# GpSimd's 512-column instructions in two parts each, and those of the weights' low halves in four

## The reference

```
x = x + 0.5 * ffn(layernorm(x), ...)
x = x + attn(layernorm(x), Wq, Wk, Wv, Wo, bo)
x = x + 0.5 * ffn(layernorm(x), ...)

attn: q, k, v = x @ Wq, x @ Wk, x @ Wv       # 32 query heads, 8 key/value groups, head size 128
      q, k = rope(q), rope(k)
      probs = softmax(where(causal, q @ k.T / sqrt(128), -inf))
      return (probs @ v) @ Wo + bo
ffn:  router scores of 128 slots, the best 8 kept, softmax over them, mixed values through two
      small matrices, times a gate made from a learned and a measured uncertainty; plus its input
```

## Time and profile before

| | |
|---|---|
| timed runs, median (lowest to highest) | 1462.56 us (1459.61 to 1463.27), 3 runs |
| the profiled execution, its own time | 1462.43 us |
| its span, first to last instruction | 1460.6 us |
| TensorE busy | 1384.1 us (95%) |
| VectorE busy | 1180.8 us (81%), 2816 instructions |
| ScalarE busy | 961.5 us (66%) |
| GpSimd busy | 721.1 us (49%), 603 instructions |
| mean granted TensorE clock | 0.978 of full |

### The profile page before, as it was taken

The page is one execution under the profiler, slowest core; times in us unless marked ns, Lnnn a source line. Parts: engine busy times, 40 slices in busy tenths (PEclk is TensorE's granted clock), DMA queues, the critical chain, the costliest instruction groups (busy, mean ns, idle before and its releaser), DMA issues.

```text
span 1460.6 us, 26285 instructions
## 1 busy us (share of the span) xinstructions
PE 1384.1 (95%) x8818; PEld 779.6 (53%) x8818; DVE 1180.8 (81%) x2816; ACT 961.5 (66%) x2423; POOL 721.1 (49%) x603
## 2 busy tenths in 40 slices
PE   5678999998999999999999999999999999999995
PEld 4335555554555655555555555555555555555543
DVE  6788968889988888889778788889777798868655
ACT  3467777676776766676766776666666777666733
POOL 0278766667765454435545354444543454344312
PEclk9699999999999999999999999999999999999997
DMA  7168766777767566656557566557565667464433
GB/s 234 44 165 205 192 158 175 191 178 196 176 144 173 135 126 134 138 119 153 129 128 167 127 134 145 119 131 141 139 138 136 135 146 161 120 141 103 98 76 116
DMA packets 439398, 210.54 MB, mean 144 GB/s; under 512 B 382016, under 2 KB 383232, under 8 KB 439264
## 3 DMA queue, kind: packets, MB, share of 16 engines
q1 hardware_dynamic: 437152, 204.66, 60.5%
q10 hardware_dynamic: 2112, 4.19, 0.9%
HBM read 90.30 MB, written 25.17 MB: 79 GB/s over the span
## 4 chain that ended last, share of the span: by engine, by line
PE 77%; DVE 11%; ACT 4%; issue 4%; POOL 3%; DMA 1%; DVEq 0%; SPq 0%; ACTq 0%
PE PJ L1191 17%; PE PJ L1193 17%; PE PJ L1192 17%; PE PV L1191 4%; PE PV L1193 4%; PE PV L1192 4%; PE SC L1357 4%; PE SC L1356 4%; PE SC L1355 4%; DVE phl L1008 3%; POOL t L530 2%; ACT p L685 2%; DVE p L998 2%; DVE t L971 1%; DVE t L969 1%
## 5 line engine op out<-in xcount | busy, mean ns | idle before, releaser
L538 POOL TENSOR_TENSOR oTl<-of,oTf 128x512 f16<-128x512 f32 x128 | 154.2, 1204 | 444.3 <-ACT oTf L677 444.2
L685 ACT ACTIVATE p<-p,mn 128x512 f32<-128x512 f32 (+3 forms) x512 | 280.8, 549 | 98.4 <-DVE mn L998 98.3
L1008 DVE SCALAR_TENSOR_TENSOR phl<-p,ri,phl 128x128 f16<-128x128 f32 (+3 forms) x512 | 333.2, 691 | 0.0
L1191 PE MATMUL PJ<-XT,wsp 128*128 128x512 f16 x640 | 244.4, 382 | 4.8 <-DVE t L971 1.7
L696 ACT ACTIVATE phl<-p,ri 128x128 f16<-128x128 f32 (+3 forms) x512 | 245.6, 550 | 4.1
L1192 PE MATMUL PJ<-XT,wsp 128*128 128x512 f16 x640 | 244.2, 382 | 0.0
L1193 PE MATMUL PJ<-XT,wsp 128*128 128x512 f16 x640 | 244.0, 381 | 0.0
L530 POOL TENSOR_TENSOR t<-t 128x512 f32<-128x512 f32 x160 | 204.7, 1279 | 72.8 <-DVE t L971 72.5
L998 DVE CUSTOM_DVE_ANT_0 p<-SC,maskw 128x512 f32<-128x512 f32 (+3 forms) x512 | 219.8, 485 | 2.1
L533 POOL TENSOR_TENSOR qTl<-t,qTh 128x512 f16<-128x512 f32 x128 | 148.4, 1159 | 93.2 <-ACT qTh L664 93.2
L1192 PE MATMUL PJ<-wosp,oTf 128*128 128x512 f16 x512 | 194.1, 379 | 0.0
(11 more groups left out here) (204 smaller groups left out, 2644.9 us busy)
## 6 DMA issues: line engine op xcount, KB each, us to landing
wsp<-kept SPq DMA_DIRECT2D x144, 256.0 KB, 3.0
wosp<-kept SPq DMA_DIRECT2D x96, 256.0 KB, 3.4
raw<-in_wqkv SPq DMA_DIRECT2D x48, 256.0 KB, 4.7
kept<-wsp SPq DMA_DIRECT2D x48, 256.0 KB, 2.4
raw<-in_wo SPq DMA_DIRECT2D x32, 256.0 KB, 4.7
kept<-wosp SPq DMA_DIRECT2D x32, 256.0 KB, 3.0
X<-in_x ACTq DMA_DIRECT2D x4, 1024.0 KB, 10.9
pTf<-phl SPq DMA_TRANSPOSE x256, 3.8
```

Of the source, the lines that this page charges most:

```text
L538: nc.gpsimd.tensor_tensor(oTl[:, n % 2, h, :], of[:, s % 2, :], oTh[:, n % 2, h, :], ALU.subtract).then_inc(o_lo, 1)
L685: ins = nc.scalar.activation(pt, pt, ACT.Exp, bias=mn[:, par, i:i + 1], scale=-1.0, accum_out=rs[:, par, i:i + 1])
L1008: nc.vector.scalar_tensor_tensor(out=phl[:, par, low(i, 0):low(i, i) + 1, :], in0=p[:, par, SOFF[i]:SOFF[i] + w].rearrange("p (k t) -> p k ...
L1191: mm(out_, lh, rh, start=start, stop=False)
```

## The change

Each GpSimd instruction over 512 columns is issued as several instructions over equal slices of the columns, one behind the other. The semaphore is raised by the last of them, so what waits for a tile waits for all of its parts, and the wait ahead of the tile is made once. Two parts of 256 columns are used for the bias addition, the low halves of normalized tiles, both rope instructions and the low half of the attention output; four parts of 128 columns for the weights. The penalty addition (L504) and the six additions at the very end (L573) stay whole. Data, order and waits stay as they are.

```diff
+            def parts(k):
+
+                return [slice(i * T // k, (i + 1) * T // k) for i in range(k)]
+
             def add_bias(bb, i):
...
-                nc.gpsimd.tensor_tensor(X[:, n, :], X[:, n, :], bob[:, :], ALU.add).then_inc(bo_add, 1)
+                for c in parts(2):
+                    ins = nc.gpsimd.tensor_tensor(X[:, n, c], X[:, n, c], bob[:, c], ALU.add)
+                ins.then_inc(bo_add, 1)
             def normal_lo(k, bb, i):
...
-                nc.gpsimd.tensor_tensor(both[:, C:2 * C], normal_of(k, bb, i), both[:, 0:C],
-                                        ALU.subtract).then_inc(ln_lo[k], 1)
+                hi, lo, x_ = both[:, 0:C], both[:, C:2 * C], normal_of(k, bb, i)
+                for c in parts(2):
+                    ins = nc.gpsimd.tensor_tensor(lo[:, c], x_[:, c], hi[:, c], ALU.subtract)
+                ins.then_inc(ln_lo[k], 1)
             def weight_low(r):
...
-                nc.gpsimd.tensor_tensor(w[:, 1, :], raw[:, r % NRAW, :], w[:, 0, :].bitcast(BF16),
-                                        ALU.subtract).then_inc(w_lo, 1)
+                for c in parts(4):
+                    ins = nc.gpsimd.tensor_tensor(w[:, 1, c], raw[:, r % NRAW, c], w[:, 0, c].bitcast(BF16), ALU.subtract)
+                ins.then_inc(w_lo, 1)
             def rope(kind, n, idx):
...
-                nc.gpsimd.tensor_tensor(t1[:, j, :], t1[:, j, :], t2[:, j, :], ALU.add).then_inc(rope_sum, 1)
+                for c in parts(2):
+                    ins = nc.gpsimd.tensor_tensor(t1[:, j, c], t1[:, j, c], t2[:, j, c], ALU.add)
+                ins.then_inc(rope_sum, 1)
...
-                nc.gpsimd.tensor_tensor(lo, t1[:, j, :], hi, ALU.subtract).then_inc(rope_lo, 1)
+                for c in parts(2):
+                    ins = nc.gpsimd.tensor_tensor(lo[:, c], t1[:, j, c], hi[:, c], ALU.subtract)
+                ins.then_inc(rope_lo, 1)
             def out_lo(s):
...
-                nc.gpsimd.tensor_tensor(oTl[:, n % 2, h, :], of[:, s % 2, :], oTh[:, n % 2, h, :],
-                                        ALU.subtract).then_inc(o_lo, 1)
+                for c in parts(2):
+                    ins = nc.gpsimd.tensor_tensor(oTl[:, n % 2, h, c], of[:, s % 2, c], oTh[:, n % 2, h, c], ALU.subtract)
+                ins.then_inc(o_lo, 1)
```

## The result

| | median us | lowest to highest | runs |
|---|---|---|---|
| before | 1461.09 | 1459.23 to 1463.27 | 4 |
| changed | 1471.11 | 1470.43 to 1471.62 | 4 |

The ratio is 1.0068, 95% interval 1.0054 to 1.0081: the change costs 10 us, where 3.5 us of gain had been forecast, and the time lies above the range of 1448 to 1468. In the changed kernel the lines of the earlier trace rows are 8 to 14 further down: L530 is now L540, L533 L545, L523 L532, L538 L552, L516 L524, and on VectorE L1008 is L1022, L844 L858 and L1102 L1116; TensorE's L1191 is L1205 and L1355 is L1369, ScalarE's L685 L699.

The account below looks back on a forecast made before the run. TensorE was taken as the bound, except before 440 us, where the loop through VectorE, GpSimd and ScalarE is as long or longer. The terms 3.8 + 0 - 7.5 + 0 + 0.2 = -3.5 us gave 1459 us, range 1448 to 1468.

Parts of the forecast that it names:

- The price of a part: On GpSimd, one more instruction adds 0.12 us, bounds 0 and 0.20; a halved instruction +0.12, a quartered one +0.36.
- Part 1: The start, 60 to 130 us: GpSimd is nearly the bound, so added instructions less idle time cost +3.8 us.
- Part 3: 250 to 440 us: shorter VectorE stalls shorten the steps and some granted clock returns, -7.5 us.
- the two chosen steps: Steps 335.88 to 348.01 and 322.93 to 335.88 us, forecast to shorten by 1.07 and 1.68 us.
- Part 2: 130 to 250 us: TensorE is the bound and GpSimd still has room, so nothing changes.
- Part 4: 440 to 1400 us: each query's rope way 0.24 us longer, TensorE busy throughout and not waiting, so nothing.
- Part 5: The end: L538 lies once before the last output products, +0.2 us.
- GpSimd becomes the bound of the early stage: Rival, chance 0.17: at 0.20 us a part, the start costs +8.4, 250 to 440 us gives -3.6: 1467 us.
- More relief: Rival, chance 0.26: a part costs only 0.05 us, start about +1, 250 to 440 us gains some 11.5: 1452 us.
- The parts do not let VectorE in: Rival, chance 0.09: GpSimd keeps its hold over the parts, stalls stay whole, only the cost is left: 1468 us.
- Hidden anyway: Rival, chance 0.06: the reciprocal waits for the exponentials and relief ends there: 1462 us.

Follow-up runs that it names:

- w4_alone: Kernel before with only the weights' low halves in four parts, everything else whole: 0.9975 of the time of the kernel before.
- w_cost_only: Kernel before with three memsets of 96 columns ahead of each weight's low half, which stays whole: ratio 1.0028 to the kernel before.
- w4_side2: Changed kernel with both rope instructions whole (weights in four; bias, normalized tiles, attention output in two): ratio 0.9999 to the kernel before.
- changed_rope_late: Changed kernel with rope sum and low half whole for the first 40 ropes, in two parts from then on: ratio 1.0009 to the kernel before.
- w2_alone: Kernel before with only the weights' low halves in two parts: 1453.07 us, ratio 0.9946 to the kernel before.
- rope2_alone: Kernel before with only the rope's sum and low half in two parts: ratio 1.0060 to the kernel before.
- side2_alone: Kernel before with only bias and low halves of normalized tiles and attention output in two parts: ratio 0.9994 to the kernel before.
- w2_side2: Kernel before with low halves of weights, normalized tiles and attention output, and bias, in two parts, rope whole: ratio 0.9972 to the kernel before.

## Why the prediction was wrong

**What held.** The price of a part was taken as 0.12 us, and is 0.14: a rope sum lasts 1.41 us against 1.27. The Trainium skill (GPSIMD Engine Reference, section Elementwise — side-by-side cycle accounting) led to an estimate of 0.17; the trace lies between the two. The parts do let VectorE in: L1022 fell to 757 ns, and w4_alone, faster than before where w_cost_only is slower, shows that this relief reaches the kernel's time.

**Part 1 agrees by luck.** It said +3.8, and +3.7 came, of which the clock at the start gave back 2.5. The four steps that it worked out one by one (sums at 93.25, 105.80, 116.71 and 128.75) were forecast at 0.5 + 0.1 + 1.7 + 0.6 = 2.9, and lost 1.2 + 0.6 + 2.3 + 0.9 = 5.0. The price of 0.14 instead of 0.12 explains 1.0 of the 2.1. The direction and the way of counting (added instructions less the idle time before the sum) hold there, and the size does not.

**The step that failed is Part 3.** It forecast -7.5 and +1.0 came. It worked out two steps by "idle time of GpSimd before the rope sum, less the price of the step's added instructions", and gave the rest of the stretch a flat 3.5 us and the clock 1.3. But the two chosen steps were those with 2.63 us of idle. Of the 32 steps whose query sums start from 76 to 411 us in the trace of before, five have 2.63; 24 have 0.5 to 1.07, two have none, and the first has 2.05. With 0.14 us for each of the 8 to 14 added instructions (fewer in some), a step with 1.07 and 12 added instructions loses 0.6 instead of gaining 0.9. The step shown above is one with 1.07: 13 added instructions, 13 x 0.14 - 1.07 = +0.75; it went from 358.80 - 348.01 = 10.79 to 363.86 - 352.16 = 11.70, +0.91. The two chosen steps themselves shortened by 0.42 and 1.10, not by 1.07 and 1.68. The granted clock of the stretch, from which 1.3 us were to come back, is 0.98 against 0.97.

I applied the same rule to all 32, after the result, with the measured price and with the idle time and the instructions of the trace of before, and compared with the two timelines:

| query sums, start before | rule, us | measured, us |
|---|---|---|
| 76 to 139 (7 steps) | +3.3 | +6.2 |
| 149 to 236 (9) | +5.2 | +3.0 |
| 247 to 411 (16) | +1.8 | +0.4 |
| all 32 (335 x 0.14 - 36.6) | +10.3 | +9.6 |

Single stages miss by 1 to 3 us, and that the sum comes so near is again a cancelling. Between the same two sums of the two traces GpSimd spent 56.4 us more in its instructions (the rule has 46.9), and idled 46.8 us less: 28.6 of the 36.6 before the query sums, 16.7 before the output's low halves, which the rule leaves out, and the rest elsewhere. The other kernels show where the rule fits and where it doesn't, each over the same 32 steps:

| kernel | added x 0.14 - 36.6 | measured, us | idle time left before the 32 sums |
|---|---|---|---|
| w4_side2 | 255: -0.9 | +1.2 | 8.8 |
| changed_rope_late | 257: -0.6 | +1.9 | 8.6 |
| w4_alone | 210: -7.2 | -3.8 | 11.4 |
| w2_alone | 70: -26.8 | -7.9 | 22.9 |
| rope2_alone | 80: -25.4 | +5.5 | 35.0 |

The rule says what a step costs when GpSimd no longer waits for VectorE before the sum. That is nearly so with the weights in four, and there the rule comes within 4 us. With the weights whole or in two most of the 36.6 us stays, and the rule says nothing. So what the runs show in place of Part 3's -7.5 is this: the parts of the weights relieve VectorE, the idle time before the sums goes from 36.6 to 8.0 us, and the added instructions use it up and more. GpSimd's share of the time did not say so; its idle time before the sums, step by step, would have said that there was little to gain.

**Part 2** said "nothing, GpSimd still has room": 84 us of 120. It had room in the window, and 0.74 to 1.07 us of it in front of each rope sum. +2.4 us came, and rope2_alone shows +3.0 there. **Part 4** said that the query's way becomes longer and TensorE does not wait for it; +1.8 came. TensorE's waits show 1.3 us of it, for the rope's products. changed_rope_late puts the parts back after the first 40 ropes and has +2.3 there, but w4_side2 and w4_alone, with no rope in parts, have 0.9 and 1.8: how much of it is the rope's can't be told from single traces. **Part 5** is within what the end moves by.

**The rivals.** "GpSimd becomes the bound of the early stage" (0.17) gave 1467 and is nearest in mechanism; 1471 is beyond it. Its deciding point, 0.16 us a part, was too high: a part costs 0.14. By the rule above, 36.6 / 335 = 0.11 us a part is where the 32 steps break even, and the 0.12 of the forecast would have given 335 x 0.12 - 36.6 = +3.6. "More relief" fell, although relief is there: w2_alone shows it, with 1453 us, where each weight pays for one part and not for three. "The parts do not let VectorE in" gave 1468, the nearest in time, and fell by its mechanism, since L1022 became shorter. "Hidden anyway" fell too.

**Why the effects do not add.** This is argued and not shown, for no run varied the idle time by itself. Each group of parts draws on the same idle time before the 32 sums: 36.6 us before, 27.1 in side2_alone, 22.9 in w2_alone, 18.9 in w2_side2, 11.4 in w4_alone, 8.8 in w4_side2. The number of sums with none goes from 2 before to 8 in w2_alone and 15 in w4_alone, and in such a step every added instruction comes on top. That fits the others' parts, which cost nothing alone and 0.0024 to 0.0026 beside the weights. It is not as simple as "free as long as it fits": a step with three weights in two has 3 x 0.14 = 0.42 us more, which leaves 0.65 of the usual 1.07 for the others' two or three, and they cost all the same. And it does not explain the rope at all: its 80 added instructions in these 32 steps are 11.2 us, the idle time before the sums stays at 35.0 of 36.6, and 5.5 us are lost. The rope's price lies on the way that the step takes (sum, cast, exponentials; low half, then the key's sum), where idle time does not take it up. Why both together cost 8.8 us where each alone costs 2.1 and 1.1 stays open.

## What to carry to other kernels

Before splitting instructions on an engine that is off the critical path, go through its steps one by one and ask two things. Does the added price lie on the way that the loop takes? Then it is lost even with idle time in front of it (the rope: 35.0 of 36.6 us of idle time left, and 1.0060). If it lies beside the loop, how much idle time is there in front of the instruction that others wait for, in most steps and not in those with the most? What was added beyond it was mostly lost here; the share of busy time over a window says nothing of this. Split only what stands beside the loop and blocks another engine (here the weights' low halves, in two: 0.9946), and leave whole what the loop passes through (the rope: 1.0060). A rule that has been worked out on two steps is to be run over all of them before its result is written down.

## What the runs showed of the hardware

One more tensor_tensor on GpSimd costs 0.14 us, for two parts of 256 columns as for four of 128. One behind the other, subtractions of 512 columns start 1.11 us apart in the kernel before, those of 256 columns 0.63 and those of 128 columns 0.38 in the changed one; 4 x 0.384 - 1.113 = 0.42 for three more. A memset of 96 columns of a 2-byte type costs 0.12 to 0.14. Two kernels that put 0.14 us more on each rope sum and rope low half, one by a split and one by a memset, give the same time within the intervals. And an engine's order is worth far more than its instructions' sizes: moving the outputs' low halves behind a wait costs 24 us, the most that any kernel here has lost without adding an instruction. TensorE's clock at the start is not the same in every execution: in 5 of the 20 traces the first projections stand 0.22 us apart from the start, in the others about 0.43 us for the first 7 to 10 of them, and that moves the first rope sum by 2.6 us between two kernels with the same program up to there (65.16 and 67.73).
